# Keeping a batch's self projection in SBUF and loading the adjacency as int8 through GpSimd's queue

## The chip, the cores and the metric

The kernel runs on one core of one Trainium2 chip. The metric is the device time of one execution in microseconds, the median of several runs.

## What is computed

```python
B, N, D = 8, 2048, 512           # x: fp32 [8, 2048, 512], adj: int32 [2048, 2048] of 0 and 1
Wi, Wj = W[:, :D], W[:, D:]
mi = x @ Wi.T                    # self projection
mj = x @ Wj.T                    # neighbour projection
a = adj.astype(float32)
deg = a.sum(axis=1)
out = deg[None, :, None] * (mi + b) + einsum('ij,bjo->bio', a, mj)
y = layernorm(x + out)           # over the last axis, eps 1e-5
```

## The kernel before

The program is written engine by engine; every order of work is the order in which the instructions stand in the block of an engine, and every dependency is a semaphore. A batch has NT = 16 tiles of 128 rows. Each batch is worked in two stages.

**Projection.** For each tile n, PE makes mj (h = 0) and then mi (h = 1). Both are products in full fp32 accuracy, put together from fp32r matmuls: four of a cross product (`cross_ps`, L341) and eight of the main product (`main_ps`, L349 and L351). Around them, ACT splits x into `x_hi` and `x_lo` (`parts`, L457, L459), POOL makes `x_df` from them (`difference`, L279), and PE needs `x_df` for the cross product of the next tile. ACT copies each cross product out of PSUM (`take_cross`, L468) into one of two buffers `cross`. DVE combines main and cross product (`combine_mj`, L597; `combine_mi`, L604). ACT rounds mj into `mj_hi` (L472), and POOL makes the rest `mj_lo` (`rest_of_mj`, L284). All 16 tiles of `mj_hi` and `mj_lo` stay in SBUF. The mi of a tile has one buffer: SP writes it to `mi_dram` in HBM (`store_mi`). The first two tiles of the program are native fp32 matmuls (`project_native`, L326), whose operands lie in buffers borrowed from later stages.

**Aggregation.** For each of the 16 output tiles PE multiplies a column block of the transposed adjacency with `mj_hi` and `mj_lo` (L373, 32 matmuls of 512 columns into one of two `agg_ps`). The block is fp32r: ACT widens it from the int8 copy `adjT8` into one of two buffers `adjT` (`widen`, L484, 128x2048), two tiles ahead, as soon as the tile that used the buffer is done. SP reads mi back (`load_mi`) into one of two buffers `mi_in`, two tiles ahead; POOL adds the bias (`add_bias`, L290); DVE makes deg * (mi + b) + x (`residual`, L632), adds the aggregate (L638), takes statistics (L640 to L642), ACT takes the root (`root`, L488), and DVE normalises (L674). Then SP stores the tile.

**The adjacency in batch 0.** `adjt` is int32 in HBM, cut into 64 chunks of 128x512. SP loads a chunk into one of AB = 4 buffers `adj_in` (`load_chunk`), ACT casts it into `adjT8` (`cast_chunk`, L479), and DVE adds it up over its 16 chunks into `deg_part` (`count_chunk`, L615 and L618). When 16 chunks are summed, PE turns them into four tiles of degrees (`degrees`, L358), and DVE copies these out (`take_degrees`). Two lists say where the counts stand:

```python
PROJ_CHUNKS = [0, 0, 2, 2, 2, 2, 2, 2, 2, 2, 2, 2, 2, 2, 2, 2]
AGG_CHUNKS = [2, 3, 3, 3, 3, 3, 3, 4, 4, 4, 4, 0, 0, 0, 0, 0]
```

So 28 chunks are counted during the projection of batch 0 and 36 in front of the sums of its first 11 output tiles. PE's `degrees` stand in the projection of tile 11 and ahead of the aggregations 3, 7 and 11. The other seven batches have no such work.

Of the kernel before, what the change touches and what calls it, by code (L numbers as in the profile page):

```python
# [5 lines left out]
def bass_adj_resnorm(nc, x, xt, adjt, wt, b, out):  # L6
# [3 lines left out]
    i32 = mybir.dt.int32  # L10
# [14 lines left out]
    AB = 4  # L25
    NG = NT // GT
    NP = NT // 2
    DH = DO // 2
# [12 lines left out]
    with ctx:  # L41
# [9 lines left out]
        mi_dram = nc.dram_tensor("mi_dram", [TILES, P, DO], fp32, kind="Internal").ap()  # L51

        adjT8 = sb("adjT8", [P, NT, N], i8)
        adjT = [sb(f"adjT{s}", [P, NT, P], fp32r) for s in range(2)]
# [20 lines left out]
        warm = sb("warm", [P, P], bf16)  # L75
# [14 lines left out]
        w_stage = [r[0], r[1], r[2], r[3], mi_in[0], mi_in[1], x_top, mi]  # L90
        x_first = [adj_in[2][:, :].bitcast(fp32), adj_in[3][:, :].bitcast(fp32)]
# [19 lines left out]
        mi_stored = sem("mi_stored")  # L111
        mi_loaded = [sem(f"mi_loaded{s}") for s in range(2)]
        r_loaded = [sem(f"r_loaded{s}") for s in range(GT)]
        adj_loaded = [sem(f"adj_loaded{s}") for s in range(AB)]
        adj_cast = sem("adj_cast")
# [6 lines left out]
        res_ready = sem("res_ready")  # L122
        agg_done = sem("agg_done")
# [12 lines left out]
        AGG_CHUNKS = [2, 3, 3, 3, 3, 3, 3, 4, 4, 4, 4, 0, 0, 0, 0, 0]  # L136
# [31 lines left out]
        def _(sp):  # L168
            def load_chunk(c):
                if c >= AB:  # L170
                    sp.wait_ge(adj_cast, c - AB + 1)
                    sp.wait_ge(deg_part_ready, c - AB + 1)
                sp.dma_start(adj_in[c % AB][:, :], adjt[c // NT, c % NT]).then_inc(adj_loaded[c % AB], 16)

            def store_mi(n):
                sp.wait_ge(mi_ready, n + 1)
                sp.dma_start(mi_dram[n], mi[:, :]).then_inc(mi_stored, 16)

            sp.dma_start(x_first[0], xt[0]).then_inc(x_first_loaded[0], 16)
            for c in range(DK + 1, 2 * DK):  # L180
                sp.dma_start(w_stage[c][:, :], wt[c]).then_inc(w_loaded[c], 16)
            sp.dma_start(x_first[1], xt[1]).then_inc(x_first_loaded[1], 16)
            for c in range(DK):
                sp.dma_start(w_stage[c][:, :], wt[c]).then_inc(w_loaded[c], 16)
# [3 lines left out]
            for c in range(2):  # L188
                load_chunk(c)
            for n in range(NATIVE):  # L190
                sp.wait_ge(main_done, NATIVE + n + 1)
                load_chunk(2 + n)
                store_mi(n)

            def load_mi(m, u):
                sp.dma_start(mi_in[u % 2][:, :], mi_dram[m]).then_inc(mi_loaded[u % 2], 16)
# [4 lines left out]
            def batch(bt):  # L201
# [4 lines left out]
                def first_loads():  # L206
                    if zero:
                        sp.wait_ge(w_ready, 2 * DK)
                        sp.wait_ge(main_done, 2 * NATIVE)
                    sp.wait_ge(mi_stored, 16 * (base + 2))  # L210
                    for u in range(2):
                        load_mi(base + u, u)
                    for u in range(GT - 1):
                        if not zero:
                            sp.wait_ge(out_stored[u], 16 * NG * bt)
                        load_r(base + u, u)

                def proj(g):
                    for u in range(GT):
                        if zero and GT * g + u < NATIVE:  # L220
                            continue
                        if zero:
                            for c in proj_chunks(GT * g + u)[:-1]:
                                load_chunk(c + AB)
                        store_mi(base + GT * g + u)
                        if zero:
                            load_chunk(proj_chunks(GT * g + u)[-1] + AB)
                        if known(g) and g == NG - 1 and u == 1:
                            first_loads()

                over_groups(sp, zero, True, proj)

                def agg(g):
                    for u in range(GT):
# [4 lines left out]
                        if begin and u == 0:  # L239
                            sp.wait_ge(mi_stored, 16 * (base + NT))  # L240
                        if not (ending and u >= GT - 2):
                            sp.wait_ge(res_ready, m + 1)
                            load_mi(m + 2, u)
# [4 lines left out]
                        if zero:  # L248
                            for c in agg_chunks(i):
                                if c + AB < CHUNKS:  # L250
                                    load_chunk(c + AB)
# [18 lines left out]

        @block.gpsimd
        def _(pool):
            pool.memset(warm[:, :], 0.0).then_inc(zeroed, 1)
# [43 lines left out]
        def _(pe):  # L317
# [73 lines left out]
            def batch(bt):  # L391
# [382 lines left out]
```

## Time and profile before

| what | value |
|---|---|
| median of 3 runs | 1642.31 us (1641.74 to 1642.79) |
| profiled execution, its own time | 1641.88 us |
| profiled execution, span | 1640.1 us |
| PE busy | 1633.5 us |
| DVE busy | 819.4 us |
| ACT busy | 660.3 us |
| POOL busy | 495.9 us |
| DMA | 187.27 MB, mean 114 GB/s |

The span is the time from the first to the last instruction of the profiled execution; the run's own time has 1.8 us around it. PE is TensorE's matmuls, PEld its weight loads, DVE VectorE, ACT ScalarE, POOL GpSimd, SP the engine that only issues transfers. The granted clock is the share of TensorE's full clock that it was given.

### The profile page before, as it was taken

What the parts mean: (1) busy time and instruction counts of PE and PEld (TensorE: products, weight loads), DVE (VectorE), ACT (ScalarE), POOL (GpSimd) and SP (SyncE); (2) the same over time, 40 slices, a digit from 0 to 9 for tenths busy, and PEclk for the clock granted to TensorE, in tenths of its full rate; (3) what the DMA queues carried; (4) which work ended last, traced back from release to release, by engine and by line L of the source; (5) the groups of instructions that cost most, each with busy time, mean ns of one, the idle gap of its engine ahead of it and who ended that gap; (6) DMA issues with size and microseconds to landing.
All of it is one profiled execution on the core that took longest, in us unless ns stands there. A gap on an engine that the chain in (4) does not pass through costs nothing.

```text
span 1640.1 us, 24474 instructions
## 1 busy us (share of the span) xinstructions
PE 1633.5 (100%) x7228; PEld 1348.6 (82%) x7228; DVE 819.4 (50%) x1745; ACT 660.3 (40%) x964; POOL 495.9 (30%) x387
## 2 busy tenths in 40 slices
PE   9999999999999999999999999999999999999998
PEld 6888888888888888888888888888888888888887
DVE  7687544454444444444444444444544444444444
ACT  6765345332453224532245332452325522255221
POOL 3431134311443114421144211442114421144210
PEclk9999999999999999999999999999999999999999
DMA  6676423433234322243223332333323333233332
GB/s 212 193 230 219 135 84 97 134 103 96 89 97 134 104 88 96 90 134 113 85 90 105 124 110 83 96 113 118 102 83 102 124 106 107 73 102 115 96 115 71
DMA packets 102843, 187.27 MB, mean 114 GB/s; under 512 B 11424, under 2 KB 11680, under 8 KB 102816
## 3 DMA queue, kind: packets, MB, share of 16 engines
q1 hardware_dynamic: 84672, 154.05, 29.5%
q10 hardware_dynamic: 18144, 32.91, 6.3%
q8 instruction: 11, 0.18, 0.0%
q14 instruction: 16, 0.13, 0.0%
HBM read 119.80 MB, written 67.11 MB: 114 GB/s over the span
## 4 chain that ended last, share of the span: by engine, by line
PE 99%; DMA 0%; DVE 0%; issue 0%; DVEq 0%; ACT 0%
PE agg_ps L373 56%; PE cross_ps L341 14%; PE main_ps L349 14%; PE main_ps L351 14%; PE main_ps L326 0%; PE cross_ps L326 0%; PE main_ps L386 0%; PE agg_ps L386 0%; DMA mi_in<-in_wt 0%; PE deg_ps L358 0%; DVE stats L655 0%; DVE r L653 0%; DVE r L674 0%; DVEq L41 0%; ACT std L488 0%
## 5 line engine op out<-in xcount | busy, mean ns | idle before, releaser
L373 PE MATMUL agg_ps<-mj_hi,adjT 128*128 128x512 f32 x2032 | 790.8, 389 | 0.0
L373 PE MATMUL agg_ps<-mj_lo,adjT 128*128 128x512 f32 x2032 | 790.5, 389 | 0.0
L484 ACT ACTIVATE adjT<-adjT 128x2048 fp32r (+1 forms) x128 | 245.3, 1916 | 569.1 <-PE agg_ps L373 569.1
L373 PEld LDWEIGHTS agg_ps<-mj_hi,adjT 128*128 128x128 f32 x2032 | 381.5, 188 | 79.3
L373 PEld LDWEIGHTS agg_ps<-mj_lo,adjT 128*128 128x128 f32 x2032 | 381.3, 188 | 79.0
L351 PE MATMUL main_ps<-W_lo,x_lo 128*128 128x512 f32 x1008 | 392.1, 389 | 0.0
L349 PE MATMUL main_ps<-W_hi,x_hi 128*128 128x512 f32 x1008 | 392.1, 389 | 0.0
L290 POOL TENSOR_TENSOR mi_in<-mi_in,bias 128x512 f32<-128x512 f32 x128 | 166.3, 1302 | 648.8 <-DMA mi_in<-mi_dram 648.8
L638 DVE TENSOR_TENSOR r<-agg_ps,r 128x512 f32<-128x512 f32 x127 | 87.9, 692 | 379.8 <-PE agg_ps L373 379.6
L341 PE MATMUL cross_ps<-W_df,x_df 128*128 128x512 f32 x1008 | 269.9, 390 | 0.0
L284 POOL TENSOR_TENSOR mj_lo<-mj,mj_hi 128x512 f32 (+1 forms) x126 | 165.9, 1317 | 325.2 <-ACT mj_hi L472 325.2
L468 ACT ACTIVATE cross<-cross_ps 128x512 f32<-128x512 f32 x252 | 148.6, 590 | 217.7 <-PE cross_ps L341 216.6
L341 PEld LDWEIGHTS cross_ps<-W_df,x_df 128*128 128x128 f32 x1008 | 189.1, 188 | 39.7 <-DVE W_df L571 0.2
L349 PEld LDWEIGHTS main_ps<-W_hi,x_hi 128*128 128x128 f32 x1008 | 189.3, 188 | 39.2
L351 PEld LDWEIGHTS main_ps<-W_lo,x_lo 128*128 128x128 f32 x1008 | 189.1, 188 | 39.3
L279 POOL TENSOR_TENSOR x_df<-x_top,x_lo 128x512 fp32r<-128x512 f32 x126 | 163.6, 1299 | 150.2 <-ACT x_lo L459 150.2
L597 DVE SCALAR_TENSOR_TENSOR mj<-main_ps,cross 128x512 f32<-128x512 f32 x126 | 87.1, 692 | 230.2 <-PE main_ps L351 224.9
L604 DVE SCALAR_TENSOR_TENSOR mi<-main_ps,cross 128x512 f32<-128x512 f32 x126 | 87.1, 691 | 108.8 <-PE main_ps L351 107.1
L632 DVE SCALAR_TENSOR_TENSOR r<-mi_in,deg,r 128x512 f32<-128x512 f32 x128 | 102.5, 805 | 12.9 <-POOL mi_in L290 9.2
L457 ACT ACTIVATE x_hi<-x_top 128x512 fp32r<-128x512 f32 x126 | 79.5, 631 | 65.3 <-PE main_ps L351 64.1
L640 DVE BATCH_NORM_STATS2 stats<-r 128x6 f32<-128x512 f32 x127 | 88.2, 695 | 11.9 <-issue 0.5
L589 DVE TENSOR_TENSOR x_raw<-x_raw,x_top 128x512 f32<-128x512 f32 x126 | 87.3, 693 | 4.3
(71 smaller groups left out, 601.9 us busy)
## 6 DMA issues: line engine op xcount, KB each, us to landing
mi_dram<-mi SPq DMA_DIRECT2D x128, 256.0 KB, 2.1
mi_in<-mi_dram SPq DMA_DIRECT2D x128, 256.0 KB, 2.7
r<-in_x SPq DMA_DIRECT2D x128, 256.0 KB, 2.7
out<-r SPq DMA_DIRECT2D x127, 256.0 KB, 2.1
x_raw<-in_xt ACTq DMA_DIRECT2D x124, 256.0 KB, 2.7
adj_in<-in_adjt SPq DMA_DIRECT2D x64, 256.0 KB, 3.6
r<-in_wt SPq DMA_DIRECT2D x4, 256.0 KB, 5.0
adj_in<-in_xt SPq DMA_DIRECT2D x2, 256.0 KB, 4.0
```

The lines of the kernel that those rows point to most:

```text
L279: pool.tensor_tensor(x_df[s][:, :], x_top[:, :], x_lo[s][:, :].bitcast(fp32), ALU.subtract).then_inc(x_df_ready, 1)
L284: pool.tensor_tensor(mj_lo[:, bass.ds(t, 1), :].rearrange("p t d -> p (t d)"), mj[:, :], mj_hi[:, bass.ds(t, 1), :].rearrange("p t d -> p ...
L290: pool.tensor_tensor(mi_in[u % 2][:, :], mi_in[u % 2][:, :], bias[:, :], ALU.add).then_inc(mib_ready, 1)
L341: last = nc.tensor.matmul(cross_ps[h][:, :], x_df[s][:, k * P:(k + 1) * P], W_df[:, half * DK + k, :], start=(k == 0), stop=(k == DK - 1))
L349: nc.tensor.matmul(main_ps[h][:, :], x_hi[s][:, k * P:(k + 1) * P], W_hi[:, half * DK + k, :], start=(k == 0), stop=False)
L351: last = nc.tensor.matmul(main_ps[h][:, :], x_lo[s][:, k * P:(k + 1) * P], W_lo[:, half * DK + k, :], start=False, stop=(k == DK - 1))
L373: last = nc.tensor.matmul(agg_ps[s][:, :], adjT[s][:, j, :], part[:, j, :], start=(j == 0 and part is mj_hi), stop=(j == NT - 1 and part i ...
L468: nc.scalar.activation(cross[h][:, :], cross_ps[h][:, :], ACT.Copy).then_inc(cross_ready, 1)
L484: nc.scalar.activation(adjT[s][:, :, :], adjT8[:, :, bass.ds(i * P, P)], ACT.Copy).then_inc(adjT_ready, 1)
L632: nc.vector.scalar_tensor_tensor(r[u][:, :], mi_in[u % 2][:, :], deg[:, bass.ds(i, 1)], r[u][:, :], ALU.mult, ALU.add).then_inc(res_ready, 1)
L638: nc.vector.tensor_tensor(r[u][:, :], agg_ps[s][:, :], r[u][:, :], ALU.add).then_inc(sum_ready, 1)
L640: nc.vector.bn_stats(stats[:, 0, :], r[u][:, :]).then_inc(ln_step, 1)
```

## The change

1. `mi` becomes one tensor of 16 tiles in SBUF. The store to HBM, the load back, `mi_dram` and the two `mi_in` are gone; `add_bias` works in place and waits for `mi_ready` alone.
2. The adjacency is loaded by POOL. One DMA (`load_pair`) takes two chunks, int32 in HBM and int8 in SBUF, straight into `adjT8`; the conversion is done on the way. `adj_in`, `cast_chunk` and SP's chunk loads are gone. `count_chunk` reads `adjT8`. Two pairs are issued ahead of the projection, one behind each `rest_of_mj` of batch 0, and the last 16 behind its `add_bias`, two each.
3. `adjT` has one buffer, widened in two halves of 128x1024. PE tells `half_done` in the middle of an aggregation, and waits there for the second half of its own tile.
4. `cross` has one buffer: `take_cross` of mi waits until mj of the same tile is combined, and `take_cross` of mj until mi of the tile before is.
5. `deg_part` has one buffer: the first chunk of a new sum waits until PE has used the last one. The counts and the `degrees` stand elsewhere (below).
6. The operands of the first matmuls lie in tiles of `mi`; SP loads the first three `r` of batch 0 at the start.

The core of the diff:

```diff
-        adjT = [sb(f"adjT{s}", [P, NT, P], fp32r) for s in range(2)]
+        adjT = sb("adjT", [P, NT, P], fp32r)
-        cross = [sb(f"cross{h}", [P, DO], fp32) for h in range(2)]
+        cross = sb("cross", [P, DO], fp32)
-        mi = sb("mi", [P, DO], fp32)
-        mi_in = [sb(f"mi_in{s}", [P, DO], fp32) for s in range(2)]
+        mi = sb("mi", [P, NT, DO], fp32)
-        adj_in = [sb(f"adj_in{s}", [P, DO], i32) for s in range(AB)]
-        deg_part = [sb(f"deg_part{s}", [P, DO], fp32r) for s in range(2)]
+        deg_part = sb("deg_part", [P, DO], fp32r)
...
-        AGG_CHUNKS = [2, 3, 3, 3, 3, 3, 3, 4, 4, 4, 4, 0, 0, 0, 0, 0]
+        AGG_CHUNKS = [4, 3, 3, 3, 3, 4, 3, 3, 3, 3, 4, 0, 0, 0, 0, 0]
...
+            def load_pair(c):
+                q, j = c // (NT // 2), 2 * (c % (NT // 2))
+                pool.dma_start(adjT8[:, j:j + 2, q * DO:(q + 1) * DO],
+                               adjt[q, j:j + 2].rearrange("j p d -> p j d")).then_inc(adj_loaded[c], 16)
+
+            pool.wait_ge(main_done, NATIVE)
+            for c in range(PAIRS_AHEAD):
+                load_pair(c)
             difference(NATIVE, 0)
...
                         rest_of_mj(n, GT * g + u)
+                        if zero:
+                            load_pair(PAIRS_AHEAD + GT * g + u - NATIVE)
...
+                    first = PAIRS_AHEAD + NT - NATIVE
+                    for i in range(NT):
+                        add_bias(i, i)
+                        for c in range(first + 2 * i, min(first + 2 * i + 2, CHUNKS // 2)):
+                            load_pair(c)
...
-                pe.wait_ge(adjT_ready, m + 1)
+                pe.wait_ge(adjT_ready, 2 * m + 1)
...
                 for j in range(NT):
+                    if j == HALF:
+                        last.then_inc(half_done, 1)
+                        pe.wait_ge(adjT_ready, 2 * m + 2)
...
-                            if zero and g == 2 and u == 3 and h == 0:
+                            if zero and g == 2 and u == 2 and h == 0:
                                 degrees(0)
...
-                        if i == 3:
+                        if i == 1:
                             degrees(1)
-                        if i == 7:
+                        if i == 6:
                             degrees(2)
...
-                act.wait_ge(mj_ready if h == 0 else mi_ready, n)
-                nc.scalar.activation(cross[h][:, :], cross_ps[h][:, :], ACT.Copy).then_inc(cross_ready, 1)
+                if h == 0:
+                    act.wait_ge(mi_ready, n)
+                else:
+                    act.wait_ge(mj_ready, n + 1)
+                nc.scalar.activation(cross[:, :], cross_ps[h][:, :], ACT.Copy).then_inc(cross_ready, 1)
...
+            def widen_behind(m, i, chunks):
+                act.wait_ge(half_done, m + 1)
+                widen(i + 1, 0, chunks)
+                act.wait_ge(agg_done, m + 1)
+                widen(i + 1, 1, None)
...
-                    if q >= 2:
-                        dve.wait_ge(deg_in_psum, q - 1)
+                    if q >= 1:
+                        dve.wait_ge(deg_in_psum, q)
```

How the instructions stand now, at two places. In the names below the number of a tensor is left out, so `adjT<-in_adjt` is a load into `adjT8`. First POOL, from the last tile of batch 0's projection into its aggregation, before:

```order
L279 TENSOR_TENSOR x_df<-x_top,x_lo 128x512 [waits x_parts_ready]
L284 TENSOR_TENSOR mj_lo<-mj,mj_hi 128x512 [waits mj_hi_ready]
L310 UNCONDITIONAL_BRANCH [waits b_loaded]
L310 ISA
L290 TENSOR_TENSOR mi_in<-mi_in,bias 128x512 [waits mi_loaded0]
L290 TENSOR_TENSOR mi_in<-mi_in,bias 128x512 [waits mi_loaded1]
```

and with the change:

```order
L227 TENSOR_TENSOR x_df<-x_top,x_lo 128x512 [waits x_parts_ready]
L232 TENSOR_TENSOR mj_lo<-mj,mj_hi 128x512 [waits mj_hi_ready]
L243 DMA adjT<-in_adjt 128x2x512
L239 TENSOR_TENSOR mi<-mi,bias 128x512 [waits mi_ready,b_loaded]
L243 DMA adjT<-in_adjt 128x2x512 x2
L239 TENSOR_TENSOR mi<-mi,bias 128x512 [waits mi_ready]
```

Each tile of the projection has gained one transfer behind `mj_lo`; the additions of the bias have lost their wait for a transfer, and two transfers stand behind each of the first eight.

Then DVE at the first output tile of batch 0 (`r<-agg_ps,r` is the sum that frees PSUM), before:

```order
L632 SCALAR_TENSOR_TENSOR r<-mi_in,deg,r 128x512 [waits deg_ready,r_loaded0,mib_ready]
L618 TENSOR_TENSOR deg_part<-deg_part,adj_in 128x512 [waits deg_part_ready,adj_loaded0]
L618 TENSOR_TENSOR deg_part<-deg_part,adj_in 128x512 [waits deg_part_ready,adj_loaded1]
L632 SCALAR_TENSOR_TENSOR r<-mi_in,deg,r 128x512 [waits deg_ready,r_loaded1,mib_ready]
L638 TENSOR_TENSOR r<-agg_ps,r 128x512 [waits agg_done,res_ready]
```

and with the change:

```order
L595 SCALAR_TENSOR_TENSOR r<-mi,deg,r 128x512 [waits deg_ready,r_loaded0,mib_ready]
L581 TENSOR_TENSOR deg_part<-deg_part,adjT 128x512 [waits deg_part_ready,adj_loaded14] x2
L581 TENSOR_TENSOR deg_part<-deg_part,adjT 128x512 [waits deg_part_ready,adj_loaded15] x2
L595 SCALAR_TENSOR_TENSOR r<-mi,deg,r 128x512 [waits deg_ready,r_loaded1,mib_ready]
L601 TENSOR_TENSOR r<-agg_ps,r 128x512 [waits agg_done,res_ready]
```

There are four counts ahead of the first sum instead of two, and the last two of them read pair 15, the one that POOL issues right behind the `mj_lo` shown above. And PE, between the first and the second output tile, with the change (before, these degrees stood two output tiles later, and nothing stood between the first two):

```order
L341 MATMUL agg_ps<-mj_lo,adjT 128x512
L323 MATMUL deg_ps<-ones,deg_part 128x2 [waits deg_part_ready]
L323 MATMUL deg_ps<-ones,deg_part 128x2 x3
L341 MATMUL agg_ps<-mj_hi,adjT 128x512 [waits adjT_ready]
```

The wait for `deg_part_ready` is for 32 counts, and the 32nd is the second of the two that wait for `adj_loaded15`.

## Rows read from the trace of the kernel before

**Rows 1.** The page: busy time and share of the span.

```profile
PE 1633.5 (100%) x7228; PEld 1348.6 (82%) x7228; DVE 819.4 (50%) x1745; ACT 660.3 (40%) x964; POOL 495.9 (30%) x387
```

**Rows 2.** The page: granted clock of PE in 40 slices of the span.

```profile
PEclk9999999999999999999999999999999999999999
```

**Rows 3.** All waits of PE (engine, line, waited for: us in total, times, longest).

```profile
PE agg_ps L429 <- POOL eps L275: 1.1, 1, 1.1
PE main_ps L326 <- DMA mi_in<-in_wt: 0.2, 1, 0.2
```

**Rows 4.** Timeline of PE (start, us, instruction) around the end of a projection tile.

```profile
67.11 0.39 PE L351 MATMUL main_ps<-W_lo,x_lo 128*128 128x512 f32 x1
67.34 1.07 PE L341 MATMUL cross_ps<-W_df,x_df 128*128 128x512 f32 x4
```

**Rows 5.** Timeline of PE where the first aggregation starts and where its second starts.

```profile
95.05 0.39 PE L373 MATMUL agg_ps<-mj_hi,adjT 128*128 128x512 f32 x1
...
102.30 0.39 PE L373 MATMUL agg_ps<-mj_hi,adjT 128*128 128x512 f32 x1
```

**Rows 6.** Timeline of POOL in the projection of batch 0 (in brackets: idle before, releaser).

```profile
61.48 1.41 POOL L284 TENSOR_TENSOR mj_lo<-mj,mj_hi 128x512 fp32r<-128x512 f32 x1 [2.24 <-ACT mj_hi L472]
63.39 1.29 POOL L279 TENSOR_TENSOR x_df<-x_top,x_lo 128x512 fp32r<-128x512 f32 x1 [0.50 <-ACT x_lo L459]
```

**Rows 7.** Timeline of POOL at the start, and of PE there.

```profile
14.86 1.71 POOL L279 TENSOR_TENSOR x_df<-x_top,x_lo 128x512 fp32r<-128x512 f32 x1 [13.84 <-ACT x_lo L459]
...
17.93 1.27 PE L341 MATMUL cross_ps<-W_df,x_df 128*128 128x512 f32 x3
```

**Rows 8.** Timeline of SP and ACT: an issue of an adjacency load, and the native drain.

```profile
86.06 0.33 SPq L173 DMA_DIRECT2D adj_in<-in_adjt  x1
...
11.66 0.60 ACT L443 ACTIVATE mj_hi<-cross_ps 128x512 fp32r<-128x512 f32 x1 [1.20 <-PE cross_ps L326]
```

**Rows 9.** The page: DMA issues (KB each, us from issue to landing), and one queue.

```profile
q1 hardware_dynamic: 84672, 154.05, 29.5%
...
adj_in<-in_adjt SPq DMA_DIRECT2D x64, 256.0 KB, 3.6
```

**Rows 10.** Timeline of DVE from the last projection tile to the first sum.

```profile
97.37 0.69 DVE L604 SCALAR_TENSOR_TENSOR mi<-main_ps,cross 128x512 f32<-128x512 f32 x1 [0.52 <-DMA mi_dram<-mi]
97.97 1.82 DVE L618 TENSOR_TENSOR deg_part<-deg_part,adj_in 128x512 fp32r<-128x512 f32 x1
99.72 0.74 DVE L632 SCALAR_TENSOR_TENSOR r<-mi_in,deg,r 128x512 f32<-128x512 f32 x1
100.38 1.48 DVE L618 TENSOR_TENSOR deg_part<-deg_part,adj_in 128x512 fp32r<-128x512 f32 x2
101.78 0.75 DVE L632 SCALAR_TENSOR_TENSOR r<-mi_in,deg,r 128x512 f32<-128x512 f32 x1
```

**Rows 11.** Timeline of POOL in the same stretch.

```profile
94.63 1.68 POOL L284 TENSOR_TENSOR mj_lo<-mj,mj_hi 128x512 fp32r<-128x512 f32 x1 [0.77 <-ACT mj_hi L472]
96.26 2.99 POOL L290 TENSOR_TENSOR mi_in<-mi_in,bias 128x512 f32<-128x512 f32 x2
```

**Rows 12.** Timeline of DVE: one whole aggregation tile of batch 0 with three counts.

```profile
124.84 0.69 DVE L638 TENSOR_TENSOR r<-agg_ps,r 128x512 f32<-128x512 f32 x1 [1.30 <-PE agg_ps L373]
...
128.06 2.28 DVE L618 TENSOR_TENSOR deg_part<-deg_part,adj_in 128x512 fp32r<-128x512 f32 x3
130.25 0.75 DVE L632 SCALAR_TENSOR_TENSOR r<-mi_in,deg,r 128x512 f32<-128x512 f32 x1
132.09 0.69 DVE L638 TENSOR_TENSOR r<-agg_ps,r 128x512 f32<-128x512 f32 x1 [1.09 <-PE agg_ps L373]
```

**Rows 13.** Timeline of ACT: a whole widening and the root behind it.

```profile
132.02 1.92 ACT L484 ACTIVATE adjT<-adjT 128x2048 fp32r<-128x2048 int8 x1 [3.54 <-PE agg_ps L373]
133.87 0.29 ACT L488 ACTIVATE std<-mean_var,eps 128x1 f32<-128x1 f32 x1
```

**Rows 14.** Timeline of DVE in the projection: the masking of x, in fp32.

```profile
65.43 0.42 DVE L586 TENSOR_SCALAR x_top<-x_raw 128x512 uint32<-128x512 uint32 x1
```

More of the change, by code:

```diff
@@ L204, in batch @@
                 base = NT * bt
[L206 to L231, printed above, removed]
+                if zero:
+                    sp.wait_ge(w_ready, 2 * DK)
+                    sp.wait_ge(main_done, 2 * NATIVE)
+                for u in range(GT - 1):
+                    if not zero:
+                        sp.wait_ge(out_stored[u], 16 * NG * bt)
+                    load_r(base + u, u)
                 def agg(g):
@@ L286, in rest_of_mj, with add_bias @@
                                    ALU.subtract).then_inc(mj_lo_ready, 1)
-            def add_bias(m, u, turn):
-                pool.wait_ge(mi_loaded[u % 2], turn)
-                pool.tensor_tensor(mi_in[u % 2][:, :], mi_in[u % 2][:, :], bias[:, :], ALU.add).then_inc(mib_ready, 1)
+            def add_bias(m, t):
+                tile = mi[:, bass.ds(t, 1), :].rearrange("p t d -> p (t d)")
+                pool.wait_ge(mi_ready, m + 1)
+                pool.tensor_tensor(tile, tile, bias[:, :], ALU.add).then_inc(mib_ready, 1)
+            def load_pair(c):
[5 more added lines that the diff above has]
+                load_pair(c)
             difference(NATIVE, 0)
@@ L309, in batch @@
                     pool.wait_ge(b_loaded, 16)
-                with pool.Fori(0, NP) as k:
-                    for u in range(2):
-                        add_bias(NT * bt + 2 * k + u, u, 16 * (NP * bt + k + 1))
+                    first = PAIRS_AHEAD + NT - NATIVE
[4 more added lines that the diff above has]
+                else:
+                    with pool.Fori(0, NP) as k:
+                        for u in range(2):
+                            add_bias(NT * bt + 2 * k + u, 2 * k + u)
             over_batches(pool, batch)
@@ L357, in degrees @@
                 for t in range(TPB):
-                    last = nc.tensor.matmul(deg_ps[:, 2 * t:2 * t + 2], deg_part[q % 2][:, t * P:(t + 1) * P], ones[:, :],
+                    last = nc.tensor.matmul(deg_ps[:, 2 * t:2 * t + 2], deg_part[:, t * P:(t + 1) * P], ones[:, :],
                                             start=True, stop=True)
@@ L372, in aggregate @@
                     for part in (mj_hi, mj_lo):
-                        last = nc.tensor.matmul(agg_ps[s][:, :], adjT[s][:, j, :], part[:, j, :],
+                        last = nc.tensor.matmul(agg_ps[s][:, :], adjT[:, j, :], part[:, j, :],
                                                 start=(j == 0 and part is mj_hi),
@@ L384, in aggregate_last @@
                     for j in range(NT):
+                        if done is first_columns_done and j == HALF:
+                            pe.wait_ge(adjT_ready, 2 * m + 2)
                         for part in (mj_hi, mj_lo):
-                            last = nc.tensor.matmul(into[:, cols], adjT[s][:, j, :], part[:, j, cols],
+                            last = nc.tensor.matmul(into[:, cols], adjT[:, j, :], part[:, j, cols],
                                                     start=(j == 0 and part is mj_hi),
@@ L473, in top_of_mj, with widen @@
                                      ACT.Copy).then_inc(mj_hi_ready, 1)
-            def cast_chunk(c):
-                s = c % AB
-                act.wait_ge(adj_loaded[s], 16 * (c // AB + 1))
-                q, j = c // NT, c % NT
-                nc.scalar.activation(adjT8[:, j, q * DO:(q + 1) * DO], adj_in[s][:, :], ACT.Copy).then_inc(adj_cast, 1)
-            def widen(i, s, chunks):
-                if chunks is not None:
-                    act.wait_ge(adj_cast, chunks)
-                nc.scalar.activation(adjT[s][:, :, :], adjT8[:, :, bass.ds(i * P, P)], ACT.Copy).then_inc(adjT_ready, 1)
+            def widen(i, h, chunks):
+                if chunks is not None:
+                    act.wait_ge(deg_part_ready, chunks)
+                rows = slice(h * HALF, (h + 1) * HALF)
+                nc.scalar.activation(adjT[:, rows, :], adjT8[:, rows, bass.ds(i * P, P)], ACT.Copy).then_inc(adjT_ready, 1)
+            def widen_behind(m, i, chunks):
[3 more added lines that the diff above has]
+                widen(i + 1, 1, None)
             def root(m):
```

114 lines of the change are left out of this document (39 added, 75 removed).

## The prediction

> **What bounds the kernel now.** I read the page's busy times first: PE is busy for 1633.5 us of a span of 1640.1, the next engine, DVE, for half of it [rows 1]. A busy PE need not be a PE at its peak, so three more views are needed. The granted clock is full in every slice [rows 2]. PE's own waits come to 1.3 us, both before its first projection [rows 3]. And the timeline gives the pitch: the first aggregation starts at 95.05 and the second at 102.30 [rows 5], 7.25 us for 32 matmuls, 0.2266 us each, with the waits at the start of a tile inside it. The whole trace is of this kind: 7,088 matmuls of 512 columns at 0.2266 us are 1606 us, and what remains is the start (the first cross product comes at 17.93 [rows 7]), the small degree products and the last tile. So PE never stops, and no edit that takes work off DMA, ACT, DVE or POOL can give time back. The change leaves PE's matmuls as they are. The question is only whether a new wait opens a hole in PE's stream.
>
> **The parts that cost nothing.** The 128 stores and 128 loads of mi go, and so do 64 casts on ACT; PE waited for none of it. A wait that is met costs PE nothing: the tile boundary in [rows 5] has one, so the 128 new waits in mid-tile cost nothing if `adjT` is ready. Is it? A whole widening is 1.92 us [rows 13], a half about 1.0. PE needs each half 3.6 us (half of 7.25) after the event that lets ACT start it. Root comes between: it starts 1.85 us after the widening does, and ACT is due again at 3.6. PE stands only if DVE brings its statistics some 4 us later than now. One `cross` buffer: ACT's copy of a cross product now waits for DVE's combination of the product before, 0.69 us [rows 10], while PE works 0.91 us (four pitches) on that cross product; both end about together, and PE wants the PSUM bank again only half a tile or more later. One `deg_part`: DVE comes to the first chunk of a new sum about 3.2 us after PE starts the degrees (124.84 to 128.06 [rows 12]). Nothing, three times.
>
> **POOL's transfers in the projection of batch 0.** No row of before has a transfer issued by POOL. Call T the time it holds POOL. Lower bound: SP's issue of one chunk, 0.33 us [rows 8]. Upper bound: POOL's own work over the same 128x1024 elements, two of its 1.3 us operations, 2.6 us [rows 6]. An issue is nearer in kind to SP's, and two chunks are two of those, 0.66; I add half for software and take T = 1.0. POOL has two limits. It works 1.41 + 1.29 = 2.7 us in a tile of 24 pitches, 5.44 us, so T may be 2.7. And `x_df`, which starts at 63.39 after `mj_lo` has ended at 62.89 [rows 6], is needed at 67.34 [rows 4]: it could end at 62.89 + T + 1.29, so T may be 3.1. With T = 1.0 both hold, 14 times. At the start, POOL waits for the native mj (11.66 [rows 8]), issues two pairs, and must have `x_df` 1.3 to 1.7 us later but before 17.93 [rows 7]: two issues may take 4.5 us. I put 0.3 us there for a first issue that is slower than the rest (0 to 2.5).
>
> The Trainium skill (DMA: Bandwidth & Descriptors, Latency and other measured facts) gives about 1 us to the first byte on the GpSimd path and 0.6 on the other. No run here shows it yet; with it as T the sum would be the same.
>
> **The boundary to the aggregation, the main term.** PE now wants 32 counts between its first and second aggregation, at 102.30. DVE had counted 30 when it came to `residual` at 101.78 [rows 10]. Two more counts are 1.4 us (1.48 for a pair, overlap off), so they end at 103.2. The wait of 0.52 for the store of mi goes: 102.7. Against that, POOL's bias additions: a count of 0.7 took 1.82 us beside them [rows 10, 11], and now a third and a fourth stand in this stretch, each of which can hold a count for up to 1.1 us. And pair 15 is issued only when `mj_lo` of the last tile ends, at 96.3 [rows 11]. A chunk lands 3.6 us after its issue [rows 9]; the second chunk of the pair is 8 more packets on each of 16 DMA engines, and a packet takes 0.295 x 16 x 1640 / 84672 = 0.091 us [rows 9], so 0.7 more; less the 0.33 of issue that T stands for, the pair lands 4.0 us after POOL has issued it. With T = 1.0 it is there at 96.3 + 1.0 + 4.0 = 101.3, about when the counts come to it; with T = 2.6 at 103, and the last count ends at 104.5. So the hole is 0.4 us without any meeting and on time, 2.2 when late, 1.2 as my value.
>
> **The rest of that aggregation.** A tile with three counts takes DVE from 124.84 to 131.0 and 0.1, 6.2 us [rows 12], with four 6.9; PE gives it 7.25. The counts of output tile 5 (four of them) must end before PE's `degrees(2)`, at the end of the same tile's aggregation: 0.2 to 1.0 us of slack, and bias additions until about tile 7. I put 0.5 us (0 to 3).
>
> Sum: 0.3 + 1.2 + 0.5 = 2.0 us on the profiled execution's 1641.9, which is 1643.9; against the median of 1642.3, **1644.3 us**. A measurement of this kernel tells 0.2%, 3.3 us, from no change; the forecast lies within it.
>
> **Rivals.**
> - *The issue on POOL is dear (slower).* T above 2.7 and each of 14 projection tiles grows. What speaks for it: engines do hold each other here (0.7 became 1.82 [rows 10]), and DVE has an operation of 0.42 us over fp32 in every tile [rows 14] and one of about 0.55 when it normalises. At T = 4: 14 x 1.26 = 17.6 us, 8 + 1.3 - 6.3 = 3 at the start, 3 at the boundary: 1666. Against it: SP's 0.33 would have to be beaten tenfold. Decides from T = 2.7. Chance 0.12. The Trainium skill (SBUF — State Buffer, A bandwidth-pool intuition that's wrong (but worth ruling out)) has a GpSimd transfer of 620 ns alone take 3100 beside a DVE copy that locks the port pair; by it T would be 3.1, 14 x 0.36 = 5 us in the projection, 1.2 at the start and 3 at the boundary, some 1651. I hold it for the low end of this rival: the operations of [rows 14] fill a tenth of a tile.
> - *The conversion slows the transfer.* A pair must land every 5.44 us. At the plain rate it fills 16 x 0.091 = 1.5 us of each engine. Should converting make it 8 us, DVE waits and PE with it, 14 x 2.6 = 36 us: about 1680. It takes a fivefold loss. Chance 0.06.
> - *DVE falls behind in batch 0's aggregation (slower).* The 16 bias additions come in one stream now, two per output tile. If each holds a count for 1.1 us, the first five tiles lose 11 us and have 4 of slack; PE stands at `degrees(2)` for the difference less what the boundary has paid, 5 or 6 us: 1649. Decides once DVE is over 1 us late at tile 5. Against it: POOL must start first each time, and DVE uses two SBUF operands in less than half of its tile. Chance 0.14.
> - *Nothing is seen.* All slack holds, 1642.3; it is within 0.2% like the forecast. Chance 0.13, with 0.52 for the forecast's hole.
> - *Faster.* Only an earlier first projection could do it, and SP issues the same loads first. 1639. Chance 0.03.
>
> **How the numbers follow.** Within 0.2% are the forecast and the unseen change, 0.65; slower the three above, 0.32; faster 0.03. The range goes from 1641.5, an unseen change with the noise of the runs, to 1653: it takes in the late DVE and the locked port, and leaves out the dear issue, the slow conversion and the faster case, under 0.2 in all.
>
> **What would show it.** Right: POOL's rows with some 1 us between `mj_lo` and the next operation; PE's waits with one new entry, on the degree products ahead of the second aggregation, for DVE's `deg_part`, 0.4 to 2.2 us; clock full; DMA traffic lower by 67 MB. Wrong: PE waiting for `x_df` (dear issue), DVE waiting for `adjT` transfers in the projection (slow conversion), PE waiting for `deg_part` at the third degrees by several us, or for `adjT` in mid-tile, which would say that root holds up the widening.

## The result

The changed kernel takes 1654.49 us (median of 6 runs, 1653.63 to 1654.9), the kernel before, measured beside it, 1642.41 us (1641.69 to 1643.24). The ratio is 1.0073 with a 95% interval of 1.006 to 1.0086: 12.1 us slower, and outside the range that was given.

### The profile after

From the page of the changed kernel: busy times, granted clock, the new queue, HBM traffic, the widening and the new transfer (KB in SBUF, us from issue to landing).

```profile
PE 1635.9 (99%) x7228; PEld 1349.8 (82%) x7228; DVE 880.6 (53%) x1745; ACT 661.6 (40%) x1028; POOL 525.1 (32%) x419
...
PEclk9999999999999999999999999999999999999999
...
q0 software_dynamic: 8704, 4.20, 3.3%
...
HBM read 86.25 MB, written 33.55 MB: 73 GB/s over the span
...
L450 ACT ACTIVATE adjT<-adjT 128x1024 fp32r (+1 forms) x256 | 271.3, 1060 | 506.3 <-PE agg_ps L341 506.3
...
adjT<-in_adjt POOLq DMA_DIRECT2D x32, 128.0 KB, 4.6
```

The bytes went as described: HBM read fell by 33.5 MB and HBM written by 33.6 MB, the mi of all batches. The rest of the page hardly tells the story. PE is still at 99%, and the clock of a slice of 41 us rounds to full. The two views that do tell it are PE's waits, where [rows 3] had nothing beyond the start:

```profile
PE agg_ps L341 <- ACT adjT L450: 7.0, 1, 7.0
PE deg_ps L323 <- DVE deg_part L581: 2.5, 1, 2.5
```

and PE's timeline (start, us; idle before and its releaser in brackets) around both:

```profile
102.13 0.39 PE L341 MATMUL agg_ps<-mj_lo,adjT 128*128 128x512 f32 x1
105.01 0.61 PE L323 MATMUL deg_ps<-ones,deg_part 128*128 128x2 f32 x4 [2.50 <-DVE deg_part L581]
...
127.14 0.39 PE L341 MATMUL agg_ps<-mj_lo,adjT 128*128 128x512 f32 x1
134.55 0.77 PE L341 MATMUL agg_ps<-mj_hi,adjT 128*128 128x512 f32 x1 [7.02 <-ACT adjT L450]
...
138.31 0.40 PE L341 MATMUL agg_ps<-mj_lo,adjT 128*128 128x512 f32 x1
```

A matmul starts at 102.13 and the next could at 102.36, but the degree products start at 105.01: 2.7 us. Another starts at 127.14, and the next at 134.55 instead of 127.37: 7.2 us. Then the matmuls follow each other slowly: the nine steps from start to start between 134.55 and 138.31 take 3.76 us where nine of 0.2266 take 2.04, so 1.7 us go. The stretches (busy time of PE, PEld, DVE, ACT and POOL, then the clock, the DMA share and GB/s) say why:

```profile
134.55:138.07 3.52, 3.52 (x8) 2.78 (x9) 3.31 (x6) 0.80 (x1) 0.00 (x0) 0.51 0.32 102
138.31:150.00 11.69, 11.69 (x53) 9.69 (x52) 10.09 (x23) 3.77 (x5) 0.00 (x0) 1.00 0.24 77
```

0.51 is the lower level, 1.2 GHz; behind 138.31 the clock is full, 2.4 GHz, again. What PE had done before it fell was to stand for 7.2 us. The three sum to 2.7 + 7.2 + 1.7 = 11.6 us, and the span has grown by 11.7 (1651.8 against 1640.1). So the whole loss lies in the first 45 us of the first aggregation, and the seven other batches cost nothing.

### Following the two holes back

The first hole waits for the 32nd count. DVE's residual and counts there (compare [rows 10]):

```profile
98.13 1.62 DVE L595 SCALAR_TENSOR_TENSOR r<-mi,deg,r 128x512 f32<-128x512 f32 x1 [1.49 <-POOL mi L239]
99.67 5.28 DVE L581 TENSOR_TENSOR deg_part<-deg_part,adjT 128x512 fp32r<-128x512 f32 x4
104.88 1.97 DVE L595 SCALAR_TENSOR_TENSOR r<-mi,deg,r 128x512 f32<-128x512 f32 x1
```

and POOL in the same stretch and on (compare [rows 11]):

```profile
94.68 1.41 POOL L232 TENSOR_TENSOR mj_lo<-mj,mj_hi 128x512 fp32r<-128x512 f32 x1 [2.03 <-ACT mj_hi L443]
96.03 0.74 POOL L243 DMA_DIRECT2D adjT<-in_adjt  x1
96.80 1.30 POOL L239 TENSOR_TENSOR mi<-mi,bias 128x512 f32<-128x512 f32 x1
...
99.50 1.39 POOL L239 TENSOR_TENSOR mi<-mi,bias 128x512 f32<-128x512 f32 x1
...
118.51 10.15 POOL L239 TENSOR_TENSOR mi<-mi,bias 128x512 f32<-128x512 f32 x8
```

Four counts took 5.28 us, where two took 1.48 before, and the residuals 1.62 and 1.97 instead of 0.74. Two of the four counts, each beside an addition, took 1.77 and 1.82 us, the other two 0.69. POOL adds a bias every 2.7 us there; before it had a pause of 4.0 us behind the second one. One row doesn't fit a simple meeting: the first residual ends at 99.75, but it began behind the first addition, and the next addition begins only at 99.50; for most of its 1.62 us POOL was issuing transfers (98.03 to 99.48). The last row is the one that matters for the second hole: behind the last transfer, eight additions in 10.15 us, some 1.25 us from one start to the next.

For the second hole, PE's row at 134.55 names ACT's widening. ACT stood for DVE, with its root ahead of the widening (compare [rows 13]):

```profile
120.31 1.06 ACT L450 ACTIVATE adjT<-adjT 128x1024 fp32r<-128x1024 int8 x1 [1.68 <-PE agg_ps L341]
133.17 0.29 ACT L460 ACTIVATE std<-mean_var,eps 128x1 f32<-128x1 f32 x1 [11.79 <-DVE mean_var L605]
133.37 1.99 ACT L450 ACTIVATE adjT<-adjT 128x1024 fp32r<-128x1024 int8 x2
```

and DVE stood in one instruction:

```profile
117.92 0.22 DVE L630 SCALAR_TENSOR_TENSOR newton<-inv,var_part 128x1 f32<-128x1 f32 x1
118.17 7.87 DVE L633 SCALAR_TENSOR_TENSOR inv_std<-newton,inv 128x1 f32<-128x1 f32 x1
126.08 1.48 DVE L637 TENSOR_SCALAR r<-r,mean_var,inv_std 128x512 f32<-128x512 f32 x1
...
132.95 0.18 DVE L605 BATCH_NORM_AGGREGATE mean_var<-stats 128x2 f32<-128x6 f32 x1
```

`inv_std` works on 128x1 elements and takes 0.16 us. Here it is recorded from 118.17 to 126.04, 7.87 us, and ends where the sixth of the eight additions does (126.02). It began 0.34 us before the first of them, beside the last issue of a transfer (117.78 to 118.50), and should have been over by 118.33; the traces don't show what held it in that first moment. Behind it everything is late: statistics at 133, root at 133.17 (ACT had been idle for 11.79 us), both halves of the widening at once, PE at 134.55.

### The profile page after: what moved, and what is told of

It reads as the page before. It is cut to its first block, busy times and chain, and to the rows that moved or that the text cites. A ratio compares the mean times of both kernels' runs of the same rounds, so it can differ in the third digit from the quotient of the medians.

```text
span 1651.8 us, 24028 instructions
## 1 busy us (share of the span) xinstructions
PE 1635.9 (99%) x7228; PEld 1349.8 (82%) x7228; DVE 880.6 (53%) x1745; ACT 661.6 (40%) x1028; POOL 525.1 (32%) x419
## 4 chain that ended last, share of the span: by engine, by line
PE 97%; DVE 2%; issue 0%; DVEq 0%; POOL 0%; ACT 0%; POOLq 0%
PE agg_ps L341 54%; PE main_ps L316 14%; PE main_ps L314 14%; PE cross_ps L306 14%; DVE inv_std L633 0%; DVE deg_part L581 0%; PE main_ps L291 0%; PE cross_ps L291 0%; PE main_ps L356 0%; PE agg_ps L356 0%; DVEq L602 0%; PE agg_ps L399 0%; DVE r L595 0%; DVE stats L603 0%; DVE deg_part L578 0%
## 5 line engine op out<-in xcount | busy, mean ns | idle before, releaser
L450 ACT ACTIVATE adjT<-adjT 128x1024 fp32r (+1 forms) x256 | 271.3, 1060 | 506.3 <-PE agg_ps L341 506.3
L239 POOL TENSOR_TENSOR mi<-mi,bias 128x512 f32 (+1 forms) x128 | 176.0, 1409 | 0.1
L568 DVE SCALAR_TENSOR_TENSOR mi<-main_ps,cross 128x512 f32 (+1 forms) x126 | 87.1, 692 | 113.5 <-PE main_ps L316 112.8
L595 DVE SCALAR_TENSOR_TENSOR r<-mi,deg,r 128x512 f32<-128x512 f32 x128 | 125.2, 982 | 15.4 <-POOL mi L239 10.9
L460 ACT ACTIVATE std<-mean_var,eps 128x1 f32<-128x1 f32 x128 | 37.7, 294 | 157.0 <-DVE mean_var L605 150.2
```

The source lines that it names most:

```text
L239: pool.tensor_tensor(tile, tile, bias[:, :], ALU.add).then_inc(mib_ready, 1)
L450: nc.scalar.activation(adjT[:, rows, :], adjT8[:, rows, bass.ds(i * P, P)], ACT.Copy).then_inc(adjT_ready, 1)
L595: nc.vector.scalar_tensor_tensor(r[u][:, :], mi[:, bass.ds(i, 1), :].rearrange("p t d -> p (t d)"), deg[:, bass.ds(i, 1)], r[u][:, :], ALU ...
```

## The experiments

The theory formed from this, P: DVE and POOL hold each other where both read SBUF, and a DVE operation with two SBUF operands cannot get in while POOL's additions follow each other; the stream of eight makes the second hole. The rivals: Q, the single `adjT` buffer behind the root turns any lateness of DVE into a wait, whatever the additions do; R, the four counts ahead of the first sum are simply too much; later D, the issue of a transfer on POOL holds DVE too. From e5_paced on, P is written P2: what holds DVE is a run of additions whose ends and starts touch, in a loop or not.

### Additions in a loop (e1_loop8)

```diff
-                    for i in range(NT):
+                    for i in range(NT // 2):
                         add_bias(i, i)
...
+                    with pool.Fori(NP // 2, NP) as k:
+                        for u in range(2):
+                            add_bias(2 * k + u, 2 * k + u)
```

> The last eight bias additions of batch 0 stand in a loop of two, as they do in the other batches, so that register instructions lie between them; the work is the same. Theory P (a DVE operation with two SBUF operands cannot get in between POOL additions that follow each other at once, and waits until the stream ends or falters): no DVE operation above 2 us there but a run of counts, the 7.0 us wait of PE for adjT goes to 0 to 1 us and the lowered clock behind it goes too, the wait for deg_part (2.5 us) stays: 1645 to 1646. Theory Q (DVE is late anyway from one addition per operation, and the single adjT buffer behind the root turns this into a wait): the wait for adjT stays at 4 us or more, 1650 to 1654. Theory R (DVE is late because of the four counts ahead of the first sum): the wait stays too, 1654.

1654.32 us, ratio 1.0072 (1.0055 to 1.0089): nothing changed. DVE's `inv_std` and POOL's additions in the timeline:

```profile
118.78 7.88 DVE L636 SCALAR_TENSOR_TENSOR inv_std<-newton,inv 128x1 f32<-128x1 f32 x1
```

```profile
119.13 10.15 POOL L239 TENSOR_TENSOR mi<-mi,bias 128x512 f32 x8
```

The loop's register instructions don't part the additions: eight still take 10.15 us. The expected gap was not there, so P's 1645 to 1646 was missed and this run tells nothing between the theories, only that the form of the loop doesn't matter.

### One transfer behind each addition (e2_one)

```diff
                         add_bias(i, i)
-                        for c in range(first + 2 * i, min(first + 2 * i + 2, CHUNKS // 2)):
-                            load_pair(c)
+                        load_pair(first + i)
```

> One transfer of the adjacency behind each of the 16 bias additions of batch 0, instead of two behind each of the first eight: the same 16 additions and 16 transfers, but every addition has a transfer of 0.73 us behind it and no stream is left. P: the wait of PE for adjT is gone, 1645 to 1646. Q and R: POOL still hits DVE's operations as often, or more often, since an addition comes every 2.0 us and not every 2.7: adjT wait of 4 us or more, 1650 to 1655.

1651.71 us, ratio 1.0059 (1.0042 to 1.0076). The wait for `adjT` is gone, as P has it, but the loss moved to the first place, as none of the theories had it; the total lies in the range of Q and R, by another wait than theirs. PE's waits, and DVE there:

```profile
PE deg_ps L322 <- DVE deg_part L580: 7.0, 1, 7.0
```

```profile
97.96 2.88 DVE L594 SCALAR_TENSOR_TENSOR r<-mi,deg,r 128x512 f32<-128x512 f32 x1 [1.49 <-POOL mi L239]
100.76 8.53 DVE L580 TENSOR_TENSOR deg_part<-deg_part,adjT 128x512 fp32r<-128x512 f32 x4
```

The first residual takes 2.88 us and four counts 8.53. An addition with one issue of a transfer (0.74 us) behind it comes every 2.0 us. In the records one of the counts, 4.18 us long, starts at 102.64 and ends at 106.83: it passes over two such issues. So the time in which POOL issues a transfer was no safe way in for DVE either. That is what theory D was made for.

### Four transfers, then twelve additions (e3_four)

```diff
-                        for c in range(first + 2 * i, min(first + 2 * i + 2, CHUNKS // 2)):
+                        for c in range(first + 4 * i, min(first + 4 * i + 4, CHUNKS // 2)):
```

> Four transfers behind each of the first four bias additions of batch 0, so that the last twelve stand in one stream (8 before). P: one DVE operation is held for 11 to 15 us (7.9 before), PE's wait for adjT grows by 3 to 6 us, 1656 to 1661. Q and R: the additions meet DVE in the same number, the wait stays within 2 us of 7.0 or shrinks, 1652 to 1655.

1655.51 us, ratio 1.0082 (1.0066 to 1.0099). DVE's longest operation and POOL's stream:

```profile
119.05 9.29 DVE L630 SCALAR_TENSOR_TENSOR newton<-inv,var_part 128x1 f32<-128x1 f32 x1
```

```profile
114.57 15.00 POOL L239 TENSOR_TENSOR mi<-mi,bias 128x512 f32<-128x512 f32 x12
```

One DVE operation is held for 9.29 us, longer than 7.87 but not the 11 to 15 expected. It is `newton`, which came in the middle of the fourth addition of the stream, and it ends with the eleventh; the three before it had met only operations with one SBUF operand, which took their usual time. So the hold need not begin where the stream does. "Two SBUF operands" isn't the whole rule of what is held, though: in the changed kernel's trace a cast with one SBUF operand took 2.01 us beside an addition, where the same cast further on (154.29) takes 0.42:

```profile
109.99 2.01 DVE L578 CAST deg_part<-adjT 128x512 fp32r<-128x512 int8 x1
```

PE's wait for `adjT` was 5.0 us: P had it grow by 3 to 6 us, and on this point Q and R are right. The clock fell twice. The total came a little below what I had written for P, and above the 1652 to 1655 of Q and R.

This trace also has DVE held where POOL only issues transfers. DVE's first residual, and POOL between its first addition and its second:

```profile
98.89 1.78 DVE L595 SCALAR_TENSOR_TENSOR r<-mi,deg,r 128x512 f32<-128x512 f32 x1 [1.50 <-POOL mi L239]
```

```profile
98.79 2.89 POOL L243 DMA_DIRECT2D adjT<-in_adjt  x4
101.68 1.53 POOL L239 TENSOR_TENSOR mi<-mi,bias 128x512 f32<-128x512 f32 x1
```

The residual takes 1.78 us instead of 0.74 and is over a full microsecond before the second addition begins. A count (1.57 us from 103.87) and another residual (1.70 us from 112.26) are held in the same way.

### The counts moved into the projection (e4_counts)

```diff
-    PAIRS_AHEAD = 2
+    PAIRS_AHEAD = 4
...
-        PROJ_CHUNKS = [0, 0, 2, 2, 2, 2, 2, 2, 2, 2, 2, 2, 2, 2, 2, 2]
-        AGG_CHUNKS = [4, 3, 3, 3, 3, 4, 3, 3, 3, 3, 4, 0, 0, 0, 0, 0]
+        PROJ_CHUNKS = [0, 0, 2, 2, 2, 2, 2, 2, 2, 2, 2, 2, 3, 3, 3, 3]
+        AGG_CHUNKS = [0, 3, 3, 3, 3, 4, 3, 3, 3, 3, 4, 0, 0, 0, 0, 0]
```

> Four pairs are issued ahead of the projection instead of two, and the last four projection tiles count three chunks each, so that all 32 counts that the second degrees need are done before the aggregation; none stands ahead of the first sum. All theories: the wait of PE for deg_part between the first two aggregations (2.5 us) goes. P: the stream of eight additions still holds one DVE operation for 6 to 9 us, but DVE comes to it 2 to 3 us earlier; PE's wait for adjT is 4 to 7 us: 1648 to 1652. R: without the counts DVE is not late and the wait for adjT goes as well: 1642.5 to 1644.

1654.78 us, ratio 1.0076 (1.0059 to 1.0093). The first hole is gone and the second is larger; the total misses P's 1648 to 1652 as well as R's range:

```profile
PE agg_ps L341 <- ACT adjT L450: 9.7, 2, 9.5
```

DVE's `inv_std` was held for 9.10 us here (118.11 to 127.21). R falls: without the four counts the hole is there. The total is the same: what the first hole no longer takes, the second takes more, since DVE and PE meet behind the same stream of additions, whenever PE arrived there.

### Additions paced by DVE (e5_paced)

```diff
                     for i in range(NT):
+                        if i:
+                            pool.wait_ge(res_ready, i)
                         add_bias(i, i)
```

> Each bias addition of batch 0 waits until DVE has made the residual of the tile before (res_ready), so no two additions follow each other. Theory P2 (what holds DVE is a run of POOL additions whose ends and beginnings touch, and loop instructions don't part them, since the loop kernel's additions were 1.27 us apart like the unrolled ones; a DVE operation loses the port at every one of these seams): no DVE operation above 3 us, PE's wait for adjT gone, no lowered clock, the wait for deg_part 1 to 2 us: 1643 to 1644.5. Theory Q (the single adjT buffer and the root ahead of it make any lateness into a wait) says 1645 or more with a wait for adjT, since DVE still works through four counts late.

1643.05 us (1642.74 to 1643.46) against 1642.30, ratio 1.0003 (0.9994 to 1.0013): 11.3 of the 12.1 us are back by one line of waits. POOL's additions now stand apart, and DVE's first residual takes its 0.75, beside two issues like those of the changed kernel:

```profile
99.79 1.30 POOL L239 TENSOR_TENSOR mi<-mi,bias 128x512 f32<-128x512 f32 x1
...
104.00 1.29 POOL L239 TENSOR_TENSOR mi<-mi,bias 128x512 f32<-128x512 f32 x1 [1.52 <-DVE r L597]
```

```profile
98.42 0.75 DVE L597 SCALAR_TENSOR_TENSOR r<-mi,deg,r 128x512 f32<-128x512 f32 x1 [1.49 <-POOL mi L239]
99.09 4.15 DVE L583 TENSOR_TENSOR deg_part<-deg_part,adjT 128x512 fp32r<-128x512 f32 x4
```

PE has one wait left, and the clock of the stretch from 95 to 211 us is full:

```profile
PE deg_ps L325 <- DVE deg_part L583: 0.5, 1, 0.5
```

Four counts take 4.15 us, of which one addition (99.79) holds one count. Q falls: DVE still has four counts there, the buffer is the single one, and no wait for `adjT` is left.

### Paced, and the counts moved (e6_counts_paced)

The edits of e5_paced and e4_counts together.

> The paced additions and the moved counts together (four pairs ahead, 32 counts in the projection). P2: none of PE's waits is left, 1642 to 1642.6, the time of the kernel before. Q: a wait for adjT stays, 1644 or more.

1642.17 us (1641.63 to 1643.03) against 1642.30, ratio 0.9999 (0.999 to 1.0009). PE waits for nothing but the start:

```profile
PE agg_ps L401 <- POOL eps L223: 1.1, 1, 1.1
```

This is the change with nothing lost. The seven other batches still have their streams of additions in it, so these cost nothing.

### The kernel before with one adjT buffer (e7_before_one_adjT)

```diff
-        adjT = [sb(f"adjT{s}", [P, NT, P], fp32r) for s in range(2)]
+        adjT = sb("adjT", [P, NT, P], fp32r)
...
+                    if j == HALF:
+                        last.then_inc(half_done, 1)
+                        pe.wait_ge(adjT_ready, 2 * m + 2)
...
-                            act.wait_ge(agg_done, i + 1)
-                            widen(i + 2, i % 2, NT * ((i + 2) // TPB + 1))
+                            widen_behind(i, i, NT * ((i + 1) // TPB + 1))
```

> The kernel before with one part of the change alone: one adjT buffer, widened in two halves, with half_done and the wait of PE in mid-tile. P2: nothing, 1642.2 (PE has no new wait, a met wait costs nothing). Q: PE waits for adjT somewhere in batch 0, where DVE has three and four counts a tile and the casts stand ahead of the widening on ACT: 1643 to 1648.

1642.87 us (1641.75 to 1643.37) against 1642.30, ratio 1.0003 (0.9993 to 1.0013), and PE has no wait but the start's 1.1 us. The halves and the 128 waits in mid-tile cost nothing.

### Short additions (e8_short)

```diff
+            def add_short(m, t):
+                pool.wait_ge(mi_ready, m + 1)
+                pool.tensor_tensor(mi[:, t, 0:1], mi[:, t, 0:1], bias[:, 0:1], ALU.add).then_inc(mib_ready, 1)
...
-                        add_bias(i, i)
+                        add_short(i, i)
```

> The changed kernel with the additions of batch 0 cut to one of 512 columns (bias is left out of the other 511 columns of batch 0); the transfers, their order and all counts stay. P2: DVE is held only for a moment, PE's wait for adjT is gone, the wait for deg_part shrinks from 2.5 to under 0.7 us: 1642.2 to 1643. Theory D (the issue of a transfer on POOL holds DVE's port as an addition does): 32 issues of 0.73 us remain, the 16 in the aggregation now without a pause, and the counts there take longer: a wait for deg_part of 1.5 us or more stays, 1644 to 1650.

1642.43 us (1641.67 to 1643.17) against 1642.30, ratio 1.0001 (0.9991 to 1.0011). PE waits for nothing new. The four counts, beside five issues of transfers by POOL:

```profile
97.65 1.48 DVE L585 TENSOR_TENSOR deg_part<-deg_part,adjT 128x512 fp32r<-128x512 f32 x2
99.73 1.49 DVE L585 TENSOR_TENSOR deg_part<-deg_part,adjT 128x512 fp32r<-128x512 f32 x2 [0.60 <-DMA adjT<-in_adjt]
```

2.97 us of work for four, and 0.60 us of waiting for pair 15. D falls as a cause of the loss by itself: with every issue in place and only the length of the additions changed, the loss is gone, and no issue held a count for anything that can be seen here. But D isn't empty either: in e3_four and in the changed kernel DVE was held beside issues with full additions around them, which happened neither here nor in e5_paced. How an issue and an addition act together isn't shown.

### Only the last eight paced (e9_last_paced)

```diff
                     for i in range(NT):
+                        if i >= NT // 2:
+                            pool.wait_ge(res_ready, i - 1)
                         add_bias(i, i)
```

> Only the last eight bias additions of batch 0 wait for DVE (each for the residual two tiles before); the first eight, with their transfers, stay as in the changed kernel. P2: the wait for adjT (7.0 us) and the lowered clock behind it go, the wait for deg_part of 2.5 us stays: 1645 us, so the stream is worth 9 of the 12 us and the first additions the rest. Q: part of the wait for adjT stays, since DVE is still late when the first eight are through: 1647 or more.

1645.68 us (1644.64 to 1648.9) against 1642.84, ratio 1.0022 (1.0013 to 1.0032). PE's only new wait:

```profile
PE deg_ps L325 <- DVE deg_part L583: 2.5, 1, 2.5
```

So the stream of eight was worth 1654.5 - 1645.7 = 8.8 us, its lowered clock included (9.2 if each kernel is taken against the kernel before measured beside it), and the first eight additions 2.8. The split is not exact: in this kernel's trace the clock fell behind the first hole of 2.7 us (eight matmuls at about 0.43 us, some 1.6 us more), in the changed kernel's it did not.

### A memset between the additions (e10_gap)

```diff
+                        if i == NT // 2:
+                            pool.wait_ge(main_done, 2 * NT)
+                        if i > NT // 2:
+                            pool.memset(x_df[1][:, 64 * (i - 9):64 * (i - 8)].bitcast(fp32), 0.0)
                         add_bias(i, i)
```

> The changed kernel with a memset of 64 columns on POOL between any two of the last eight additions (it reads nothing and takes some 0.1 us), and no wait for DVE. If any operation that doesn't read is enough of a gap, DVE gets in at the first one: no DVE operation above 2.5 us, the wait for adjT gone, 1645. If DVE is held because it loses the port at every seam whatever lies in it, the hold of 8 us stays and is longer by the memsets: 1654 to 1656.

1651.16 us, ratio 1.0052 (1.0035 to 1.0068): between the two. POOL and DVE:

```profile
120.02 1.48 POOL L239 TENSOR_TENSOR mi<-mi,bias 128x512 f32<-128x512 f32 x1
121.45 0.14 POOL L274 MEMSET x_df<- 128x64 f32 x1
121.55 1.65 POOL L239 TENSOR_TENSOR mi<-mi,bias 128x512 f32<-128x512 f32 x1
```

```profile
118.77 1.60 DVE L641 TENSOR_SCALAR r<-r,mean_var,inv_std 128x512 f32<-128x512 f32 x1
120.29 5.17 DVE L585 TENSOR_TENSOR deg_part<-deg_part,adjT 128x512 fp32r<-128x512 f32 x3
```

With 0.14 us of memset between them, DVE gets in at every gap: `r` in 1.60, three counts in 5.17. No operation is held for more than one addition. That part of the expectation held, but not the time: one addition for nearly every DVE operation is still about 1 us each, and PE waits 4.2 us for `deg_part` (in two places) and 0.9 for `adjT`. With the gaps there was no long hold; what was left went only in the kernels that set the additions apart (e5_paced) or made them short (e8_short). That the memset is what let DVE in is likely and not shown, since in batches 1 to 7 DVE gets in without one (below).

## Why the prediction was wrong

- **PE never stops, nothing to gain:** right. No version here is faster than 1642.2, and removing 67 MB of HBM traffic and 64 casts gave nothing.
- **The parts that cost nothing:** right. A half is 1.06 us (about 1.0 forecast), e7_before_one_adjT shows it, and e6_counts_paced has one `cross`, one `deg_part` and one `adjT` at the time of the kernel before.
- **POOL's transfers in the projection:** right in kind, a little high in size. POOL is held for 0.74 us by a pair (forecast T = 1.0), the very first one for 0.86, and PE waits nowhere for `x_df`: its first aggregation starts at 95.10 where it started at 95.05, so the 0.3 us for the start was not needed. Landing took 4.6 us from issue (forecast 5.0 with T in it). The later issues stay at 0.72 to 0.77 in every run, but for one of 0.84 in e3_four. The 3.1 us that the Trainium skill (SBUF — State Buffer, A bandwidth-pool intuition that's wrong (but worth ruling out)) gives for a GpSimd transfer beside a DVE copy did not appear in any run here.
- **The boundary:** mechanism right, size off. Forecast 1.2 us (0.4 to 2.2), measured 2.5 in PE's waits and 2.7 in its starts. The sum had 0.4 us without a meeting and 1.2 as its value, so it left 0.8 us for everything else. Ahead of the 32nd count the first residual and two of the four counts were held, for 0.9, 1.1 and 1.1 us; the second residual comes behind that count. The late pair, the other reason for a larger hole, did not happen: pair 15 was issued at 96.03, a pair lands 4.6 us after its issue, and the first count that reads it began at 102.35.
- **"The rest of that aggregation", 0.5 us (0 to 3):** this is the step that failed. In its place stand the second hole and the slow clock behind it, 7.2 + 1.7 = 8.9 us. The step looked only at the counts of output tile 5, and put the additions at two per output tile until about tile 7; in fact eight of them, with no transfer between them, ran in 10.15 us and were over by 128.66, ahead of output tile 4. And an addition was priced everywhere as a hold of at most 1.1 us, from one meeting in the trace of before. I had listed the additions as one stream in a rival, and even counted 16 of them, but gave each its own price. Six in a row held one operation. And the hold struck the chain that leads to ACT's root, for which I had written that PE stands if DVE is 4 us late, without asking what could make it so.
- **The rival "DVE falls behind":** it named the stream, with a chance of 0.14; its place and time (5 or 6 us at `degrees(2)`, 1649) were wrong for the same reason. PE stood for `adjT` behind root, ahead of output tile 4.
- **Not in the sum at all:** what a hole does to the clock, 1.7 us. The prediction expected a full clock.

**What stays open.** In batches 1 to 7 additions follow each other just as closely, and DVE gets in at each seam. For batch 1, DVE in the timeline:

```profile
321.21 0.85 DVE L630 SCALAR_TENSOR_TENSOR newton<-inv,var_part 128x1 f32<-128x1 f32 x1
322.10 1.22 DVE L633 SCALAR_TENSOR_TENSOR inv_std<-newton,inv 128x1 f32<-128x1 f32 x1
323.35 1.48 DVE L637 TENSOR_SCALAR r<-r,mean_var,inv_std 128x512 f32<-128x512 f32 x1
```

Each operation waits for one addition, 1.0 us or so, and then runs. Why DVE lost five to seven seams in a row in batch 0 (in four kernels, three times with `inv_std` of the same tile and once with `newton`) and none here is not settled; the form of POOL's loop is not it (e1_loop8). One difference stands in the traces: only in batch 0 does POOL issue transfers among or just ahead of its additions, and every hold longer than one addition lies there. From 215 us on no DVE operation takes more than 1.78 us in any of the runs. A stream of additions in batch 0 with no transfer of POOL's ahead of it was not tried. That the length of the additions and their distance decide is shown (e8_short, e5_paced); that it is their reading of SBUF which holds DVE is argued from e10_gap alone.

## What to carry to other kernels

A wait that is removed from a helper engine may have been its pacing: here the load of mi from HBM had kept POOL's additions 7 us apart, and without it they came in one stream beside DVE. When one engine's operations hold up another's, as POOL's did DVE's here, ask for its work in a row and not for its sum, and give it a wait on the progress of the engine it disturbs: a `wait_ge` on `res_ready` ahead of each addition brought back 11.3 of 12.1 us. Where PE is at its bound, look only for holes, and price a hole of several microseconds with the slow clock behind it.

## What the runs showed of the hardware

- An operation of DVE of 0.16 or 0.22 us with two SBUF operands was held for 7.87 to 9.29 us in four kernels, beside POOL tensor operations that started some 1.25 us apart. The Trainium skill (SBUF — State Buffer, Who interferes with whom) says that a DVE instruction with two SBUF inputs contends with a GpSimd instruction that reads SBUF; the trace agrees (a count of 0.69 us took 1.77 beside an addition). Its rule that whoever issues first has the pair for the whole instruction (given there for DVE's two-port modes), applied here, would end the hold with the addition in progress, after 1.3 us at most; the measurement differs.
- With a POOL operation of 0.14 us that reads nothing between any two additions, DVE got in behind each of them (e10_gap). In batches 1 to 7 it did so without.
- A DVE residual of 0.74 us took 1.78 while POOL only issued transfers (e3_four), and 0.75 beside such issues in e5_paced and e8_short.
- A DMA that turns int32 into int8 on the way costs POOL 0.74 us for 256 rows of 512 elements and lands 4.6 us after its issue, beside 3.6 for a plain one of half the source bytes [rows 9].
- The clock was at 0.51 for 3.5 us behind a hole of 7.2 us. Behind holes of 1.9 to 2.7 us it fell in three kernels (e3_four, e9_last_paced, e10_gap), and behind 2.7 us it stayed full in the changed kernel and e1_loop8.
